# GpSimd adds a bias row to y in SBUF, and the last 36 slots of the schedule are laid out anew

## The reference, cut to what matters

```python
out1 = einsum(sparsemax(scale * (x @ Wq + bq) @ keys), values) @ Wo + bo
y    = layernorm(x + out1)
s    = y @ Win + bin_                          # 512 -> 64
h    = relu(s[..., None] * W1 + b1)            # 16 inner values per channel
g    = einsum('btmh,mh->btm', h, W2) + b2
out  = layernorm(y + g @ Wout + bout)          # bout: one row of 512
```

## Time and profile before

| what | value |
|---|---|
| time, median of 3 runs | 1397.43 us (1396.17 to 1398.07) |
| the profiled execution: time, span | 1396.98 us, 1395.2 us |
| PE busy, share of the span | 1298.3 us, 93% |
| PEld | 854.7 us, 61% |
| ACT | 1167.7 us, 84% |
| DVE | 1108.5 us, 79% |
| POOL | 660.7 us, 47% |
| DMA queue, share of 16 engines | 56.6% |

### The profile page before, as it was taken

One profiled execution on the slowest core, in us unless ns is written; L12 is line 12 of the kernel. 1 busy time (PEld: TensorE's weight loads), 2 busy tenths in 40 slices (PEclk: granted clock), 3 DMA queues, 4 the chain that ended last, 5 costly groups with the idle time before them and its releaser, 6 DMA issues. The chain is left out here.

```text
span 1395.2 us, 28156 instructions
## 1 busy us (share of the span) xinstructions
PE 1298.3 (93%) x7118; PEld 854.7 (61%) x7118; DVE 1108.5 (79%) x4547; ACT 1167.7 (84%) x2640; POOL 660.7 (47%) x1642
## 2 busy tenths in 40 slices
PE   6981989999999999999999999999999999999974
PEld 5650566666676666666666666666766666554442
DVE  2986887898888888888888888888888888754554
ACT  2660756789999999999999999999999999988883
POOL 1330333345555555555455555555555554545544
PEclk9995999999999999999999999999999999999995
DMA  5380786555565555555555655655655555577743
GB/s 180 90 216 12 175 232 205 182 182 173 191 206 178 200 204 176 204 197 177 209 190 181 212 183 189 212 179 192 207 177 200 195 181 201 186 237 257 249 118 72
DMA packets 91849, 258.33 MB, mean 185 GB/s; under 512 B 15731, under 2 KB 15731, under 8 KB 75286
## 3 DMA queue, kind: packets, MB, share of 16 engines
q1 hardware_dynamic: 91670, 256.39, 56.6%
HBM read 206.00 MB, written 50.33 MB: 184 GB/s over the span
## 5 line engine op out<-in xcount | busy, mean ns | idle before, releaser
L619 PE MATMUL bank<-G_sb,pT 128*128 128x512 f32 x1024 | 460.7, 593 | 0.0
L619 PEld LDWEIGHTS bank<-G_sb,pT 128*128 128x128 f32 x1024 | 184.9, 191 | 183.4 <-issue 183.4
L1041 DVE SCALAR_TENSOR_TENSOR acc<-hinge,w2c,acc 128x512 f32<-128x512 f32 x224 | 167.6, 748 | 107.5 <-ACT hinge L734 107.3
L999 DVE MAX8 top<-bank 128x8 f32<-128x32 f32 x2048 | 212.5, 182 | 38.8 <-issue 38.7
L431 POOL TENSOR_TENSOR shift_sq<-sum,per_row_sq 128x1 f32<-128x1 f32 x256 | 89.3, 349 | 248.7 <-DVE y_sb L893 248.5
L734 ACT ACTIVATE hinge<-s_sb,b1c,w1c 128x512 f32<-128x512 f32 x256 | 206.0, 808 | 0.0
L548 PE MATMUL bank<-A_hi,xT_lo 128*128 128x512 f32 x512 | 203.7, 398 | 0.0
L546 PE MATMUL bank<-A_hi,xT_hi 128*128 128x512 f32 x512 | 203.6, 398 | 0.0
L547 PE MATMUL bank<-A_lo,xT_hi 128*128 128x512 f32 x512 | 203.4, 397 | 0.0
L719 ACT ACTIVATE unread<-y_sb,shift_sq 128x512 bf16<-128x512 f32 x256 | 184.0, 719 | 18.7 <-POOL minus_mean L433 18.7
L893 DVE SCALAR_TENSOR_TENSOR y_sb<-bank,y_sb 128x512 f32<-128x512 f32 x256 | 169.2, 663 | 13.4 <-PE bank L646 13.1
(11 more groups left out here) (119 smaller groups left out, 2536.7 us busy)
## 6 DMA issues: line engine op xcount, KB each, us to landing
G_sb<-G_of_heads SPq DMA_DIRECT2D x128, 1024.0 KB, 5.4
x_sb<-in_L_attn_query_dram SPq DMA_DIRECT2D x128, 256.0 KB, 4.7
y_sb<-in_L_attn_query_dram SPq DMA_DIRECT2D x256, 128.0 KB, 5.4
out_dram<-o_sb SPq DMA_DIRECT2D x256, 128.0 KB, 4.7
G_of_heads<-y_sb SPq DMA_DIRECT2D x64, 256.0 KB, 3.9
y_sb<-in_L_attn_Wk_dram SPq DMA_DIRECT2D x1, 1024.0 KB, 5.6
y_sb<-in_L_attn_Wq_dram SPq DMA_DIRECT2D x1, 1024.0 KB, 8.4
y_sb<-in_L_attn_Wv_dram SPq DMA_DIRECT2D x1, 1024.0 KB
```

The costliest lines, as they stand in the source:

```text
L619: mm = nc.tensor.matmul(o_ps[i % 2][:], pT[:, bass.ds(pair_place(turn, i) + (i % H * C + c) * P, P)], G_sb[:, i % GR, c, :], start=(c == 0 ...
L999: mx = nc.vector.max(top8[:, h, :], z_ps[i % 2][:, h * S:(h + 1) * S])
L1041: nc.vector.scalar_tensor_tensor(acc[:], hinge[:, k % HR, :], w2c[:, k:k + 1], acc[:], ALU.mult, ALU.add).then_inc(s_acc, 1)
```

## The change

GpSimd gets a new instruction in each slot, `LAG_BOUT` 27: once the tile's y is transposed it adds `bout_bc` to the tile's rows in `y_sb`. `bout_bc` is bout loaded into all 128 partitions. The place in GpSimd's order is behind the two `norm` calls and `acc_lo`, ahead of the two `mean` calls. The second residual waits for this addition (`s_yb`) where it waited for the transposes. TensorE's bias matmul L643 goes, and with it the memset and the two VectorE instructions that made `bout_rows`.

In the drain:

- for tiles from 102 on (slots 128 and later) s goes to the bank `xT_ps`, which the x transposes have left, so the y transposes no longer wait for ScalarE's s; they wait for y and for the previous `yT`.
- for odd tiles from 110 on (slots 144 and later) f goes to the bank `uT_ps`, so two banks alternate.
- y's normalisation and `yT` move from ScalarE to VectorE, from slot 128 on.
- the last group's 8 hinges and 8 steps run four to a slot in slots 154 and 155 instead of two to a slot in 154 to 157; its split is in slot 156 instead of 158, into memory of its own, and its lower half is taken by VectorE.

```diff
+LAG_BOUT = 27
-        bout_rows = sb("bout_rows", [P, D], F32R)
+        bout_bc = sb("bout_bc", [P, D])
...
+        LAST = TILES - GROUP
+        ALONE_S = TILES - LAG_YT
+        ALONE_F = TILES + UNROLL - LAG_OUT
+        def s_place(i):
+            return xT_ps if i >= ALONE_S else ys_ps
+        def f_place(i):
+            return uT_ps if i >= ALONE_F and i % 2 else f_ps
+        def hinges(turn, j, half):
+            n = turn * UNROLL + j - LAG_HINGE
+            lead, q = n - n % GROUP, n % GROUP
+            if 0 <= lead < LAST:
+                return [(lead, 2 * q + half)]
+            if lead == LAST and 2 * q < GROUP:
+                return [(lead, 4 * q + 2 * half), (lead, 4 * q + 2 * half + 1)]
+            return []
+        def split_lead(turn, j):
+            n = turn * UNROLL + j - LAG_SPLIT
+            if n == LAST - 2:
+                return LAST
+            return n if 0 <= n < LAST and n % GROUP == 0 else None
...
-                (bout_row, bout.rearrange("(a d) -> a d", a=1)),
+                (bout_bc[:], bout.rearrange("(a d) -> a d", a=1).broadcast_to([P, D])),
...
+                if in_range(turn, j, LAG_BOUT):
+                    i = j - LAG_BOUT
+                    pool.wait_ge(s_yT, base + i + 1)
+                    nc.gpsimd.tensor_tensor(y_sb[:, i % YR, :], y_sb[:, i % YR, :], bout_bc[:],
+                                            ALU.add).then_inc(s_yb, 1)
...
-                        pe.wait_ge(s_sc, 4 * (base + i))
+                    if base + i >= 1:
+                        pe.wait_ge(s_yTc, base + i)
+                        if s_place(base + i - 1) is ys_ps:
+                            pe.wait_ge(s_sc, 4 * (base + i))
...
-                        pe.wait_ge(s_r2, base + i)
+                        pe.wait_ge(s_r2, base + i - 1 if base + i > ALONE_F else base + i)
-                    nc.tensor.matmul(f_ps[:], pick_c[:], bout_rows[:], start=True, stop=False)
+                    nc.tensor.matmul(f[:], hi[:, here], Wout_hi[:], start=True, stop=False)
...
+                if split_lead(turn, j) == LAST:
+                    dve.wait_ge(s_acchi, TILES // GROUP)
+                    nc.vector.tensor_tensor(last_lo, acc[:], last_hi.bitcast(F32), ALU.subtract).then_inc(s_acclo, 1)
+                if in_range(turn, j, LAG_YT) and vector_finishes(turn):
+                    i = j - LAG_YT
+                    dve.wait_ge(s_yT, base + i + 1)
+                    dve.wait_ge(s_s, base + i)
+                    dve.wait_ge(s_yTc, base + i)
+                    nc.vector.tensor_copy(yT[:].rearrange("p c n -> p (c n)"), ys_ps[:]).then_inc(s_yTc, 1)
...
+                if in_range(turn, j, LAG_Y) and vector_finishes(turn):
+                    i = j - LAG_Y
+                    dve.wait_ge(s_y, base + i)
+                    dve.wait_ge(s_shift1, base + i + 1)
+                    nc.vector.tensor_scalar(y_sb[:, i % YR, :], y_sb[:, i % YR, :], rstd1[:, i % 2:i % 2 + 1],
+                                            shift1[:, i % 2:i % 2 + 1], ALU.mult, ALU.add).then_inc(s_y, 1)
```

More of the change, by code:

```diff
@@ L254, in vector_finishes, with split_of @@
             return isinstance(turn, int) and turn >= TILES // UNROLL
+        LAST = TILES - GROUP
[18 more added lines that the diff above has]
+            return n if 0 <= n < LAST and n % GROUP == 0 else None
+        def split_of(lead):
+            return (last_hi, last_lo) if lead == LAST else (acc_hi[:], acc_lo[:])
         def so_far(turn, j, lag):
@@ L628, in slot @@
                             tokens = slice(t * HALF, (t + 1) * HALF)
[L629 removed]
+                            mm = nc.tensor.matmul(s_ps[t * M:(t + 1) * M, 0:HALF], Win_sb[:, c, :],
                                                   yT[:, c, tokens], start=(c == 0), stop=(c == C - 1))
@@ L723, in make_hinge @@
             def make_hinge(turn, j, half):
[L725 to L735, removed]
+                for lead, k in hinges(turn, j, half):
+                    g = lead // GROUP
+                    if k == 0:
+                        act.wait_ge(s_sc, 4 * (lead + GROUP))
+                    if lead > 0 or k >= HR:
+                        act.wait_ge(s_acc, g * KH + k - HR + 1)
+                    nc.scalar.activation(hinge[:, k % HR, :], s_sb[:, g % 2, :], ACT.Relu,
+                                         bias=b1c[:, k:k + 1], scale=w1c[:, k:k + 1]).then_inc(s_hinge, 1)
             def slot(turn, j):
@@ L749, in slot @@
                             nc.scalar.activation(s_sb[half, par, q * P + t * HALF:q * P + (t + 1) * HALF],
-                                                 ys_ps[rows, 0:HALF], ACT.Identity,
+                                                 s_ps[rows, 0:HALF], ACT.Identity,
                                                  bias=bin_sb[rows, :]).then_inc(s_sc, 1)
[L752 to L758, removed]
+                lead = split_lead(turn, j)
+                if lead is not None:
+                    act.wait_ge(s_acc, (lead // GROUP + 1) * KH)
+                    if 0 < lead < LAST:
+                        act.wait_ge(s_f, lead)
+                    nc.scalar.copy(split_of(lead)[0], acc[:]).then_inc(s_acchi, 1)
                 if in_range(turn, j, LAG_COUNT):
@@ L780, in slot @@
                                          ).then_inc(s_final, 1)
-                if in_range(turn, j, LAG_Y):
+                if in_range(turn, j, LAG_Y) and not vector_finishes(turn):
                     i = j - LAG_Y
@@ L792, in slot @@
                     nc.scalar.copy(xT_hi[:].rearrange("p c n -> p (c n)"), xT_ps[:]).then_inc(s_xhi, 1)
-                if in_range(turn, j, LAG_YT):
+                if in_range(turn, j, LAG_YT) and not vector_finishes(turn):
                     i = j - LAG_YT
@@ L1025, in hinge_step @@
             def hinge_step(turn, j, half):
[L1027 to L1042 removed]
+                for lead, k in hinges(turn, j, half):
+                    g = lead // GROUP
+                    dve.wait_ge(s_hinge, g * KH + k + 1)
+                    if k == 0:
+                        if lead > 0:
+                            dve.wait_ge(s_acclo, g)
+                        nc.vector.tensor_scalar(acc[:], hinge[:, k % HR, :], w2c[:, k:k + 1], b2c[:],
+                                                ALU.mult, ALU.add).then_inc(s_acc, 1)
+                    else:
+                        dve.wait_ge(s_acc, g * KH + k)
+                        nc.vector.scalar_tensor_tensor(acc[:], hinge[:, k % HR, :], w2c[:, k:k + 1],
+                                                       acc[:], ALU.mult, ALU.add).then_inc(s_acc, 1)
             slots(dve, slot)
```

51 lines of the change are left out of this document (19 added, 32 removed).

## The result

The changed kernel takes 1373.18 us (median of 4 runs, 1372.29 to 1374.66) beside 1397.72 us of the kernel before in the same job (4 runs, 1396.17 to 1398.07): ratio 0.9828, 95% interval 0.9811 to 0.9845. The prediction was 1368 us, range 1353 to 1382. The profiled execution took 1374.66 us with a span of 1372.9, against 1396.98 and 1395.2 before, so the two traces differ by 22.3 us of span. The profiled execution was the slowest of the four, 1.5 us above their median, and the profiled executions of the kernels further down lie up to 2.4 us to either side of their medians. So a difference of two spans can be off by as much, and where the medians say something else both are given.

The account below looks back on a forecast made before the run. TensorE was taken to bound the even stretch. Gains of 21.6 us there, 1 at the start, 4.7 in the drain and 2.0 in the tail sum to 29.3, from 1396.98 to 1367.7; predicted 1368 us, range 1353 to 1382.

Parts of the forecast that it names:

- The even stretch and the start: Slots 34 to 127 gain 0.23 us each, 21.6 us; fewer setup instructions gain 1 us at the start.
- that rival: Even stretch: L643's longer step was its own, so 0.32 us a slot, 1360 us in all; chance 0.07.
- The addition in the even stretch: GpSimd's addition takes 1.25 us; its lock costs VectorE 0.1 to 0.3 us a slot of 0.59 spare, so nothing is lost.
- one of my signs of being wrong: Even stretch: the prediction is wrong if VectorE waits for GpSimd's lock there.
- one sign of being right: Even stretch: VectorE's waits for ScalarE go down by the 0.23 us a slot and no more.
- DVE takes PE's place: Even stretch: an addition blocks VectorE every slot; 1383 us in part (chance 0.10), 1430 in full (0.03).
- The drain, slots 136 to 149: Eleven plain slots gain 0.67 us each, three with `acc_lo` lose 1.33 each: 3.4 us gained.
- The drain runs at PE's pace: Drain: the addition slips into gaps, slots take TensorE's 5.41 us; 1354 us in all; chance 0.12.
- The drain gives nothing or loses: Drain: locks hold plain slots at 6.2 us and `acc_lo` slots at 7.9; 1381 us in all; chance 0.16.
- slots 128 to 135: First drain slots: 2.2 us gained, less 1 us for VectorE's `yT` behind the scores in slot 128: 1.2 gained.
- the same two chains: Drain: ScalarE and GpSimd's cycle, 5.5 us in a plain slot; the chain through `acc_lo` and the addition, 7.9 us.
- Slots 150 to 153 and the tail: Slot 150 loses 1.3 us, 152 and 153 gain 0.7 each, 0.1 together; the tail gains 2.0.

Follow-up runs that it names:

- the doubled addition: Changed kernel with a second GpSimd addition of the same size, written to spare memory, in every slot below 128: 1385.11 us, one run.
- the later takeover: Changed kernel, but ScalarE keeps y's normalisation and `yT` up to slot 131, not 127: 1372.94 us, ratio 0.9821.
- the kernel with the drain alone: Changed kernel with the matmul for bout kept on TensorE and no addition on GpSimd: 1384.26 us, ratio 0.9907.
- the kernel with the addition alone: Kernel before, with the addition of bout on GpSimd and L643 gone, the drain as it was: 1387.27 us, ratio 0.9932.

## Why the prediction was right, and which terms were not

The time came 5 us above the forecast (1373.2 against 1368) and inside the narrower range of 1361 to 1375 too. The mechanism held in full in the even stretch, which gave what was said, and gave the whole gain. The drain and the tail, from slot 128 on, were to give 6.7 us and gave nothing (206.6 us before, 206.7 after): most of their parts behaved as told, but one stage lost what the others won.

**The even stretch and the start: right.** 94 slots by 0.23 us and 1 us were 22.6; the trace has 22.5, of which the start is 0.7. The 0.23 for L643, chosen over 0.32, is what the slots show, so that rival falls.

**The addition in the even stretch: right, with less room than it looked.** I took 1.25 us from `acc_lo` and the overlap; the median is 1.29, and the estimate of 1.12 us was too short, since no addition took less than 1.26. I allowed VectorE 0.1 to 0.3 us a slot for the lock, and it was 0.32, within the 0.59 that it had. That VectorE works from PSUM at that point was true of part of its instructions, and those kept their time; the hinge step, `u_sb` and two small ones got longer. So one of my signs of being wrong was met to the letter (VectorE held up by GpSimd in the even stretch), and one sign of being right was missed (its waits down by 0.23 us and no more). Neither was well chosen: such a delay costs nothing while VectorE has waits left. TensorE has no gap with one addition and has gaps with two. *DVE takes PE's place* is therefore not what happened, but the doubled addition shows that it was one more such instruction away.

That GpSimd's work lengthens those VectorE instructions shows in the rows that run side by side, 1.72 us for `u_sb` in the even stretch, 1.69 in slot 129 and 1.09 and 1.51 in slot 142, and in the 29.9 us by which VectorE is less busy without the addition. By the Trainium skill, SBUF — State Buffer, section "Who interferes with whom", the two engines exclude each other at their shared ports; every one of these rows agrees. In these four rows the VectorE instruction got longer by 0.55 to 1.03 us, which is 0.1 to 0.3 us less than what was left of the GpSimd instruction.

**The drain, slots 136 to 149: right in its parts.** Plain slots were to take 5.5 us and take 5.31; slots with `acc_lo` 7.9, and they take 8.2, of which 3.28 are ScalarE's wait for GpSimd, as told. The addition ahead of `acc_lo` gives 1.4 us of each such slot back, which shows its place as the cause. *The drain runs at PE's pace* was near for the plain slots (5.41) and wrong for the others. *The drain gives nothing or loses* says the sum of drain and tail about as well as my forecast (they lost 0.2 us; it had 6 lost, I had 6.7 gained; that the time still fell in my range is in part luck), but not its reason, since the plain slots were not held at 6.2.

**The step that failed: slots 128 to 135.** The prediction had them in one sentence, "by the same two chains I get 2.2 us gained, less 1 us", and they lost 5.1. That is 6.3 of the 7.0 us by which the profiled run missed the forecast (29.3 said, 22.3 of span). The 2.2 does not follow from the two chains as they stand either: six plain slots at 0.67 gained and two with `acc_lo` at 1.33 lost give 1.4. Three things stand in its place. First, slot 129 takes 3.5 us more than before: VectorE's `yT` stands behind the last tiles' scores and a blocked hinge step, and not in slot 128 only, as I had it; without the addition it still takes 10.61 us, with the later takeover it is back at 8.76. Second, slot 132 takes 2.3 us more, which is what the eight matmuls take over 3.60: the lower clock behind a wait of 2.76 us. The prediction has no term for the clock at all. Third, the two slots with `acc_lo`, 130 and 134, take 2.0 and 0.9 more, where I had reckoned 1.3 for each. Against them stand 3.6 us won in the other four. The addition's share of this stage is 5.4 us (without it 58.28), of which 1.4 is clock, since the eight matmuls take 4.51 us there.

What sets the clock's fall is not settled. In nine kernels (all that were run with the changed drain but two) the wait ahead of those eight matmuls was 1.7 to 2.8 us and they took 4.51 to 6.05; in the kernel with the drain alone the wait at the same place was 2.26 us and they took 3.60, and with s in the shared bank it hardly waited there. Nor does one length of wait decide: in the kernel with the addition alone TensorE waited 2.1 us in slots 139, 143 and 147, and only behind the last was the clock low. Nothing was tried on this alone.

**Slots 150 to 153 and the tail: 1.2 and 0.8 us too good.** Slot 150 with `acc_lo` takes 8.19, and slots 152 and 153, which were to gain 0.7 us each, gain 0.3 and 0.1. In the tail the first sum of squares comes 5.03 us behind s (I had 4.98), but the second 10.0 behind it (8.6): the four hinges take 0.82 us each and ScalarE waits 0.97 more for GpSimd. The later steps are shorter than said, five of 2.51 us and one of 2.80 where I had 2.7. OUT of tile 124 comes 16.65 us behind s of slot 154, 3.8 sooner than before and not 5.

**The sum by experiments.** The addition alone gives 10.1 us and the drain alone 13.1 (medians, beside 1397.35); together 23.2, and the whole change gives 24.5. The two parts nearly add up, though one edit of the drain, s's own bank, is worth 21 us once the addition and the other edits are there. Which of the other edits of the drain (the second bank of f, the last group's hinges four to a slot) gives what was not tried.

## What to carry to other kernels

A pass moved off the bound engine pays its step in the stretch where that engine is the bound, and can cost more than it pays where another engine's chain sets the pace; where one trip of the loop is written out, do the move by tile (here the late tiles kept their matmul, for 10.9 us more on top of 24.5). In an order that an engine works through, put the new instruction where the engine waits anyway, here ahead of `acc_lo` and not behind it: the same instruction at the other place cost 8 to 10 us more (medians and spans). When several edits of a schedule are made together, take them away one by one: here one bank carried all the others. And when a stage changes hands, add up its first slots one by one: the steady slot says nothing of them.

## What the runs showed of the hardware

An addition of 128x512 on GpSimd made VectorE's instructions longer, with no semaphore between them: by 0.32 us a slot in the mean, single ones from 0.69 to 1.72 us, from 0.75 to 1.69 and from 0.54 to 1.51. Those of VectorE with one input from a bank kept their mean (0.69 and 0.69, 0.66 and 0.65). The addition itself took 1.26 us at least and up to 1.83.

TensorE ran eight matmuls of 128x512 in 3.60 us at a granted clock of 1.00, and in 5.91 at 0.53 behind a gap of 2.76 us; within a microsecond behind them it was at 1.00 again. So a wait of 2 to 3 us in a drain may cost nearly that much again, or nothing, as in the kernel with the drain alone (2.26 us of wait, 3.60 for the eight).
